# A low-rank feed-forward and the attention behind it: who computes the low parts of ctx, when the second half is turned, and what waits for both halves

## The reference

```python
def _L2_ffn_ref(x, A, B, Wr, br):          # H = 8 heads, rank r = 16
    router_logits = jnp.einsum('bsd,hd->bsh', x, Wr) + br
    scores = H * jax.nn.softmax(router_logits, axis=-1)
    low = jnp.einsum('bsd,hrd->bshr', x, A)
    out = jnp.einsum('bshr,hor,bsh->bso', low, B, scores)
    return SCALING * out                    # SCALING = 2

def _L3_xattn_ref(k, q, v):                 # k = v = ctx, q = layernorm(x)
    scores = jnp.einsum('bcn,bcm->bnm', k, q) / jnp.sqrt(jnp.float32(input_dim))
    attn = jax.nn.softmax(scores, axis=-1)
    return jnp.einsum('bnm,bcm->bcn', attn, v)
```

## Time and profile before

| what | value |
|---|---|
| median of the three runs | 1137.8 us (1135.73 to 1139.4) |
| the profiled execution, its own time | 1140.02 us |
| its span, first to last instruction | 1138.2 us |
| PE busy | 958.2 us (84%) |
| DVE busy | 731.0 us (64%) |
| ACT busy | 470.2 us (41%) |
| POOL busy | 407.1 us (36%) |
| mean granted TensorE clock | 0.904 |
| the touched stage | 854 to 988 us of the span |

### The profile page before, as it was taken

One profiled execution on the slowest core, in us unless ns is written; L12 is line 12 of the kernel. 1 busy time (PEld: TensorE's weight loads), 2 busy tenths in 40 slices (PEclk: granted clock), 3 DMA queues, 4 the chain that ended last, 5 costly groups with the idle time before them and its releaser, 6 DMA issues. The chain is left out here.

```text
span 1138.2 us, 15083 instructions
## 1 busy us (share of the span) xinstructions
PE 958.2 (84%) x5011; PEld 632.0 (56%) x5011; DVE 731.0 (64%) x1180; ACT 470.2 (41%) x687; POOL 407.1 (36%) x371
## 2 busy tenths in 40 slices
PE   5888884999999999999846788899887588769997
PEld 2555542756666666664424556444473355447886
DVE  5577557396778687756878953577643788444434
ACT  2355432325666566652345432344402455335130
POOL 5244212205767565642235720100020432137531
PEclk7699875999999999999977898899987799879999
DMA  8000103135987957547112100000003010022001
GB/s 308 1 1 2 57 1 120 53 130 185 345 290 279 385 202 259 203 151 251 60 65 93 56 1 1 20 1 1 1 1 149 0 47 1 1 74 93 19 20 38
DMA packets 33421, 112.70 MB, mean 99 GB/s; under 512 B 4352, under 2 KB 4672, under 8 KB 30656
## 3 DMA queue, kind: packets, MB, share of 16 engines
q1 hardware_dynamic: 25824, 87.08, 20.9%
q0 software_dynamic: 7520, 24.65, 6.4%
HBM read 132.69 MB, written 16.78 MB: 131 GB/s over the span
## 5 line engine op out<-in xcount | busy, mean ns | idle before, releaser
L1200 POOL DMA_INDIRECT f_picks<-f_turn_xn,f_target x47 | 113.4, 2413 | 73.2 <-ACT f_turn_xn L1089 72.9
L1616 PE MATMUL banks<-f_t_dn,f_z 128*128 128x512 f32 x188 | 88.5, 593 | 0.6 <-issue 0.6
L1344 DVE TENSOR_TENSOR f_gu_lo<-f_t_gu,f_gu_hi 128x2048 fp32r<-128x2048 f32 x24 | 55.2, 2298 | 15.7 <-ACT f_gu_hi L1075 13.4
L1194 POOL DMA_INDIRECT f_turn_xn<-f_xn_rows,f_token x47 | 47.6, 1012 | 43.6 <-DVE f_token L1338 18.7
L1344 DVE TENSOR_TENSOR f_xn_lo<-f_t_gu,f_xn_hi 128x2048 fp32r<-128x2048 f32 x23 | 52.7, 2292 | 14.7 <-ACT f_xn_hi L1075 14.7
L106 POOL TENSOR_TENSOR a_ahead_var_eps<-mean_var,eps 128x1 f32<-128x1 f32 x16 | 3.0, 190 | 161.4 <-DVE mean_var L102 161.4
L2341 ACT ACTIVATE a_e<-banks 128x1024 f32<-128x1024 f32 x32 | 32.7, 1023 | 51.8 <-PE banks L2440 51.7
L1082 ACT ACTIVATE f_sil<-banks 128x256 f32<-128x256 f32 x47 | 18.0, 384 | 78.2 <-PE banks L247 78.2
L1075 ACT CAST f_gu_hi<-f_t_gu 128x2048 fp32r x24 | 45.7, 1904 | 10.7 <-DMA f_t_gu<-in_f_gu 8.2
L164 PE MATMUL banks<-ident,f_turn_xn 128*128 128x128 f32 x96 | 21.6, 379 | 33.8 <-DVE f_turn_xn L172 33.8
L1075 ACT CAST f_xn_hi<-f_t_gu 128x2048 fp32r x23 | 43.7, 1902 | 10.6 <-DMA f_t_gu<-in_f_gu 7.9
(11 more groups left out here) (426 smaller groups left out, 2760.7 us busy)
## 6 DMA issues: line engine op xcount, KB each, us to landing
f_t_gu<-in_f_gu SPq DMA_DIRECT2D x47, 1024.0 KB
f_t_dn<-in_f_dn SPq DMA_DIRECT2D x47, 512.0 KB, 4.5
f_t_gu<-f_picks SPq DMA_DIRECT2D x8, 1024.0 KB, 5.1
f_xn_rows<-f_turn_xn SPq DMA_DIRECT2D x9, 256.0 KB, 2.2
x_res<-in_x SPq DMA_DIRECT2D x8, 256.0 KB, 7.6
a_ctx<-in_ctx SPq DMA_DIRECT2D x2, 1024.0 KB, 13.8
a_out_mask<-in_mask SPq DMA_DIRECT2D x1, 2048.0 KB, 16.0
a_ct<-in_ctx_turned SPq DMA_DIRECT2D x4, 512.0 KB, 7.1
```

Source lines behind the costliest of these rows:

```text
L1194: pool.indirect_dma_start(t_rows[:, t % F0_BUFS, :], None, dram["f0_xn_rows"], bass.IndirectOffsetOnAxis(ap=token[:, t:t + 1], axis=0))\
L1200: pool.indirect_dma_start(dram["f0_picks_flat"], bass.IndirectOffsetOnAxis(ap=target[:, t:t + 1], axis=0), t_y[:, t % F0_BUFS, :], None).t ...
L1344: dve.tensor_tensor(t_gu_lo[t % 2], t_gu[:, bass.ds(i, 1), :, :].rearrange("p i c n -> p (i c n)"), t_gu_hi[t % 2].bitcast(F32), ALU.subtr ...
L1616: mm = pe.matmul(ps[:, TY_BANK + t % 2, :], t_zt[:, t % 2, c, :], t_dn[:, t % F0_BUFS, c, :], start=c == 0, stop=c == F0_IC - 1)
```

## The change

Seven edits, all in this stage:

- The second half's turns are threaded into `lower(0)`: batches 4 and 5 are turned ahead of it, batches 6 and 7 between its second and its third chunk of four. ACT's `take_low(0)` goes behind the casts of batches 4 to 7.
- ctx is no longer split by `Weights`: ACT casts piece 0 between `take_low(0)` and `take_logit(1)` and piece 1 between the exponential of the router and `take_low(1)`.
- The low parts of ctx are made by DVE in four units of two batches: `ctx_lo(0)` ahead of the router's softmax, `ctx_lo(1)` behind the widening, `ctx_lo(2)` ahead of `add_low(0)`, `ctx_lo(3)` behind `maximum(0)`. `scores` waits for a unit every second batch.
- The low part of weight B is made by DVE (`subtract`), ahead of the normalization of batch 5, and no longer by POOL.
- The halves of `low` are waited for apart: `times_low(0)`, `times_low(1)`, `low_rest(0)`, and `low_rest(1)` only behind `add_low(0)`.
- `query(0)` goes ahead of `add_low(1)`, and the first query's low part is made by DVE (`first_query_lo`) behind `add_low(1)`.
- SP loads the two ctx pieces without waits between them, and the next stage's weights once the four units are done.

```diff
--- before.py
+++ after.py
@@ -234,6 +234,14 @@
             else:
                 pool.tensor_tensor(lo, self.raw[:, i % 2, 0:src.shape[1]], hi.bitcast(F32),
                                    ALU.subtract).then_inc(self.lo_ready, 1)
+
+    def subtract(self, dve, pieces):
+        for i in pieces:
+            src, hi, lo = self.pieces[i]
+            dve.wait_ge(self.hi_ready, i + 1)
+            dve.wait_ge(self.lo_ready, i)
+            dve.tensor_tensor(lo, self.raw[:, i % 2, 0:src.shape[1]], hi.bitcast(F32),
+                              ALU.subtract).then_inc(self.lo_ready, 1)
 
     def wait(self, pe, i):
         pe.wait_ge(self.lo_ready, i + 1)
@@ -2551,11 +2559,10 @@
         c_hi = sbuf(nc, lay, "a3_c_hi", [P, B, D], F32R)
         c_lo = sbuf(nc, lay, "a3_c_lo", [P, B, D], F32R)
         v = [sbuf(nc, lay, f"a3_v{h}", [P, NC, HT]) for h in range(HALVES)]
-        pieces = []
-        for h in range(HALVES):
-            batches = slice(h * HB, (h + 1) * HB)
-            pieces.append((dram["ctx_rows"][h], chunked(c_hi[:, batches, :]), chunked(c_lo[:, batches, :])))
-        ctx = Weights(core, "a3", pieces, core.raw)
+
+        ctx_loaded = [core.sem(f"a3_ctx_loaded_{h}") for h in range(HALVES)]
+        ctx_hi_ready, ctx_lo_ready = core.sem("a3_ctx_hi_ready"), core.sem("a3_ctx_lo_ready")
+        UNITS, PER_UNIT = 4, B // 4
         v_loaded = [core.sem(f"a3_v_loaded_{h}") for h in range(HALVES)]
         xn = sbuf(nc, lay, "a3_xn", [P, 2, D])
         q_hi = sbuf(nc, lay, "a3_q_hi", [P, 2, D], F32R)
@@ -2596,10 +2603,12 @@
                 sp.dma_start(br[:, :], dram["f2_br"]).then_inc(br_loaded, 16)
 
                 sp.wait_ge(weights.lo_ready, len(weights.pieces))
-                ctx.load(sp)
+                for h in range(HALVES):
+                    sp.dma_start(core.raw[:, h, :], dram["ctx_rows"][h]).then_inc(ctx_loaded[h], 16)
                 for h in range(HALVES):
                     sp.dma_start(chunked(v[h][:, :, :]), dram["ctx_turned"][h]).then_inc(v_loaded[h], 16)
-                ctx.prefetch(sp)
+                sp.wait_ge(ctx_lo_ready, UNITS)
+                core.prefetch(sp, "a3", None)
 
             @block.gpsimd
             def _(pool):
@@ -2616,13 +2625,10 @@
                     pool.tensor_tensor(q_lo[:, b % 2, :], xn[:, b % 2, :], q_hi[:, b % 2, :].bitcast(F32),
                                        ALU.subtract).then_inc(q_lo_ready, 1)
 
-                weights.split_lo(pool, [1])
                 pool.memset(scales[:, :], scale).then_inc(scales_set, 1)
-                ctx.split_lo(pool, [0])
                 pool.wait_ge(scales_set, 1)
                 middle_scale(0)
                 middle_scale(1)
-                query_lo(0)
                 for b in range(B):
                     if b + 1 < B:
                         query_lo(b + 1)
@@ -2630,8 +2636,6 @@
                         ahead.scale(pool, b - 2)
                     if b + 2 < B:
                         middle_scale(b + 2)
-                    if b == 0:
-                        ctx.split_lo(pool, [1])
                 ahead.scale(pool, B - 2)
                 ahead.scale(pool, B - 1)
 
@@ -2653,6 +2657,10 @@
                     if b >= 2:
                         act.wait_ge(scores_done, NC * (b - 1))
                     act.copy(q_hi[:, b % 2, :], xn[:, b % 2, :]).then_inc(q_hi_ready, 1)
+
+                def ctx_hi(h):
+                    act.wait_ge(ctx_loaded[h], 16)
+                    act.copy(chunked(c_hi[:, h * HB:(h + 1) * HB, :]), core.raw[:, h, :]).then_inc(ctx_hi_ready, 1)
 
                 def exp(j):
                     act.wait_ge(shift_ready, j + 1)
@@ -2673,18 +2681,18 @@
                 weights.split_hi(act, [1])
                 act.wait_ge(br_loaded, 16)
                 take_logit(0)
+                turned.act(act, range(HB, B))
                 take_low(0)
-                turned.act(act, range(HB, B))
+                ctx_hi(0)
                 take_logit(1)
                 act.wait_ge(shifted_ready, 1)
                 act.activation(weight[:, :, :], weight[:, :, :], ACT.Exp).then_inc(weight_exp, 1)
+                ctx_hi(1)
                 take_low(1)
-                ctx.split_hi(act, [0])
                 for h in range(HALVES):
                     act.wait_ge(lt_ready, h + 1)
                     act.copy(lt_hi[:, rows_of(h)], lt[:, rows_of(h)]).then_inc(lt_hi_ready, 1)
                 query_hi(0)
-                ctx.split_hi(act, [1])
                 for j in range(A3_JOBS):
                     exp(j)
                     if j >= 1:
@@ -2720,6 +2728,30 @@
                     dve.tensor_scalar(xn[:, b % 2, :], core.x[:, b, :], middle.mean(b), rstd[:, b:b + 1],
                                       ALU.subtract, ALU.mult).then_inc(xn_ready, 1)
 
+                def first_query_lo():
+                    dve.wait_ge(q_hi_ready, 1)
+                    dve.tensor_tensor(q_lo[:, 0, :], xn[:, 0, :], q_hi[:, 0, :].bitcast(F32), ALU.subtract)\
+                       .then_inc(q_lo_ready, 1)
+
+                def ctx_lo(u):
+                    h, part = divmod(u, UNITS // HALVES)
+                    batches = slice(u * PER_UNIT, (u + 1) * PER_UNIT)
+                    dve.wait_ge(ctx_hi_ready, h + 1)
+                    dve.tensor_tensor(chunked(c_lo[:, batches, :]),
+                                      core.raw[:, h, part * PER_UNIT * D:(part + 1) * PER_UNIT * D],
+                                      chunked(c_hi[:, batches, :]).bitcast(F32), ALU.subtract).then_inc(ctx_lo_ready, 1)
+
+                def times_low(h):
+                    dve.wait_ge(low_ready, h + 1)
+                    dve.wait_ge(wide_turned, h + 1)
+                    dve.tensor_tensor(lt[:, rows_of(h)], low[:, rows_of(h)], ps[:, G_BANK + h, :],
+                                      ALU.mult).then_inc(lt_ready, 1)
+
+                def low_rest(h):
+                    dve.wait_ge(lt_hi_ready, h + 1)
+                    dve.tensor_tensor(lt_lo[:, rows_of(h)], lt[:, rows_of(h)], lt_hi[:, rows_of(h)].bitcast(F32),
+                                      ALU.subtract).then_inc(lt_lo_ready, 1)
+
                 def maximum(j):
                     dve.wait_ge(scores_done, j + 1)
                     dve.tensor_reduce(shift[:, j:j + 1], ps[:, S_BANK + j % 2, :], AX.X, ALU.max,
@@ -2743,7 +2775,10 @@
 
                 turned.dve(dve, range(0, 2))
                 weights.first_lo(dve)
-                turned.dve(dve, range(2, B))
+                turned.dve(dve, range(2, HB + 1))
+                weights.subtract(dve, [1])
+                turned.dve(dve, range(HB + 1, B))
+                ctx_lo(0)
                 dve.wait_ge(logits_turned, 1)
                 after(dve.tensor_reduce(col[:, :], by_row(), AX.X, ALU.max))
                 dve.tensor_tensor(weight[:, :, :], by_row(), by_batch(col), ALU.subtract)\
@@ -2758,21 +2793,21 @@
                     batches = slice(h * HB, (h + 1) * HB)
                     w = weight[:, batches, :].unsqueeze(3).broadcast_to([P, HB, F2_H, F2_R])
                     dve.tensor_copy(wide[:, batches, :, :], w).then_inc(wide_ready, 1)
-                dve.wait_ge(low_ready, HALVES)
-                for h in range(HALVES):
-                    dve.wait_ge(wide_turned, h + 1)
-                    dve.tensor_tensor(lt[:, rows_of(h)], low[:, rows_of(h)], ps[:, G_BANK + h, :],
-                                      ALU.mult).then_inc(lt_ready, 1)
-                for h in range(HALVES):
-                    dve.wait_ge(lt_hi_ready, h + 1)
-                    dve.tensor_tensor(lt_lo[:, rows_of(h)], lt[:, rows_of(h)], lt_hi[:, rows_of(h)].bitcast(F32),
-                                      ALU.subtract).then_inc(lt_lo_ready, 1)
+                ctx_lo(1)
+                times_low(0)
+                times_low(1)
+                low_rest(0)
+                ctx_lo(2)
                 add_low(0)
+                low_rest(1)
+                query(0)
                 add_low(1)
-                query(0)
+                first_query_lo()
                 for j in range(A3_JOBS):
                     b, n = divmod(j, NC)
                     maximum(j)
+                    if j == 0:
+                        ctx_lo(3)
                     if j >= 1:
                         invert(j - 1)
                         divide(j - 1)
@@ -2789,8 +2824,8 @@
 
             @block.tensor
             def _(pe):
-                def product(out, cols, h):
-                    for c in range(NC):
+                def product(out, cols, h, chunks=range(NC)):
+                    for c in chunks:
                         mm = matmul_split(pe, out, a_hi[:, c, cols], a_lo[:, c, cols],
                                           hi[:, c, rows_of(h)], lo[:, c, rows_of(h)], c == 0, c == NC - 1)
                     return mm
@@ -2799,8 +2834,10 @@
                     pe.wait_ge(turned.lo_ready, HB * (h + 1))
```

(16 more changed lines are left out.)

## The result

| | before | changed kernel |
|---|---|---|
| median of the four runs of each | 1138.6 us (1135.73 to 1141.37) | 1121.2 us (1116.63 to 1125.67) |
| ratio | | 0.9837, 95% interval 0.9801 to 0.9873 |
| profiled execution, own time; span | 1140.02; 1138.2 us | 1125.67; 1123.9 us |
| stages ahead (same code) | 853.97 us | 856.08 us |
| touched stage, first DVE instruction to the next stage's | 134.90 us | 120.81 us |

The account below looks back on a forecast made before the run. The feed-forward was taken as bound by a chain from engine to engine, no engine full. Terms -10.0 (to scores(0)), +1.2 and -4.2 sum to -13.0 us, from 1137.8 to 1124.8 us; own range 1121 to 1128, reaching 1120.5 to 1130.5.

Parts of the forecast that it names:

- Parts 1 and 2: Turns amid lower(0), with PE's clock staying full through logits(1): the router's first DVE step 5.0 us earlier.
- rival of a falling clock: logits(1) runs at 1.2 GHz as before, costing 2.4 us, total 1127.2 us; chance 16%.
- Part 3: Casts and low parts of ctx put into waits: hidden, margins 0.55 us (cast) and 0.7 us (unit 0); a unit 1.22 us.
- Parts 4 and 5: ACT's cast and POOL's subtraction out of the way of f_lt's splitting, ahead of low_output(0): -0.9 and -3.9 us.
- Part 6: From low_output(0) to scores(0): -0.5 us for matmuls at full clock, +0.4 for low_rest(1) holding POOL; scores(0) 10.0 us earlier.
- Part 7: Unit 3 of ctx's low parts behind maximum(0) in the attention: +1.2 us, bounds 0.7 and 2.3.
- Part 8: POOL's second subtraction gone from the attention, between maximum(4) and maximum(8): -4.2 us, bounds -2.5 and -4.5.

Follow-up runs that it names:

- e5: Kernel before with one line moved: ACT casts ctx piece 0 ahead of take_logit(1), POOL still making the low part; ratio 0.9934 to the kernel before.
- e8: Changed kernel plus a useless POOL subtraction of two unrelated SBUF tiles ahead of its first scaling; low_rest(0) 4.54 us instead of 0.69, touched stage 125.15 us.
- e12: Changed kernel unaltered, third set of timings; 1125.5 us against 1142.2 for the kernel before, ratio 0.9835; touched stage 122.58 us.
- e9: Changed kernel plus two useless POOL memsets ahead of its first scaling; touched stage 120.76 us, stage behind 149.69 us.
- e10: Changed kernel plus one useless DVE subtraction of 448 columns ahead of the stage's last add; 1125.1 us, ratio 0.9879 to the kernel before.
- e1: Changed kernel unaltered, run again for a second set of timings; 1125.6 us against 1139.9 for the kernel before, ratio 0.9882.
- e4: Kernel before with only the second half's turns put amid lower(0) and take_low(0) behind the casts; ratio 0.9967 to the kernel before.
- e11: Changed kernel plus two useless DVE subtractions of 1024 columns ahead of the stage's last add; 1129.5 us, ratio 0.9908 to the kernel before.
- e7: Changed kernel with add_low(1) and query(0) ahead of low_rest(1), and ctx_lo(3) ahead of the first maximum; 1121.1 us against 1138.1 for the kernel before, ratio 0.9849.

## Why the prediction was wrong

Parts 1 and 2, -5.0 for the router: -5.05 in the profile, -5.02 and -4.94 when put back or made alone. The rival of a falling clock didn't come: `logits(1)` ran at 1.00 (rows above). Part 3: the cast and unit 0 were hidden, with margins of 0.57 and 0.74 us (0.55 and 0.7 worked out); a unit takes 1.22 us, as interpolated. Parts 4 and 5, -4.8: -4.89 in e5. In the changed kernel `low_output(0)` came 37.93 - 27.96 = 9.97 us earlier, 9.8 worked out. Part 6: `scores(0)` -10.4, not -10.0. `low_rest(1)` did hold POOL (0.47 - 0.19 = 0.28 us, taken 0.4). Part 7, +1.2 for unit 3: 0.89. Part 8, -4.2: from 12.52 to 7.91 us, -4.6; I had followed these jobs to 8.3, and the lower bound that I gave, -4.5, was passed by 0.1. Together the touched stage came to -14.1, 1.1 more than the sum; all three terms, parts 6, 7 and 8, erred to the same side. The mechanism of the touched stage was right in each part. Two things in the working don't hold as written. The rule of two SBUF inputs is said to speak for part 8 too, but the division has one tensor input (see e8); its price rested on the rows, and came. And the range's own terms, taken all at once, give 1121.8 to 1129.9, so the 1121 given for "not all at once" lies outside even that, and the reach to 1120.5 had no term under it.

The step that failed stands behind the sum: "From then on the loop is as before, and so is the next stage". The loop was, to 0.02 us; the next stage was not. It took 2.3 us less in the first profile (149.33 to 147.01), and 2.0 to 2.4 less in the two other profiles of the changed kernel. With it the sum would have been -13.0 - 2.3 = -15.3, or -16.4 with the stage's measured 14.1. The prediction puts that term at nothing with the reason that the stage's weights land far ahead, and it costs the clock only where the change has instructions. What the runs showed in its place: the stage behind takes 146.9 to 149.7 us, in step with when its clock comes up, 3.3 to 6.7 us after its start. With e12's slower touched stage among them, the three profiles of the changed kernel give (14.1 + 14.1 + 12.3) / 3 = 13.5 us there and 2.3 behind, 15.8 in all; the three sets of timings gave 17.4, 14.3 and 16.6, 16.1 on average.

The second step is "1.8 us to either side by which the runs shown differ from their median". Three runs showed 3.7 us of width; 24 runs later showed 11.7 (1134.29 to 1146.03), from stages whose code is the same. The rest of the first result's 17.4 us, over these 15.8, is within that. Which part of that spread a set of four runs catches is luck: the second set's 14.3 would have lain within the range. Whether the 2.3 us behind would stay in a mean over many runs is open, as e9 and e10 show. Why the stages ahead take 849 us in one run and 857 in the next was not taken apart: their granted clock differs from run to run (0.82 to 0.91 in the first two stretches of 150 us), but what sets it stays open.

## What to carry to other kernels

A subtraction of two SBUF tiles on DVE and one on POOL don't run side by side: look for a DVE instruction that takes 4.5 us where its like takes 0.7, and move the long one into a wait, even if nothing else changes (e5: 4.9 us at `low_output(0)` and 3.9 at the stage's end, for one line moved). Where PE's clock rises and falls in a stage, a later stage of unchanged code can take 2 to 3 us more or less (147.29 in e1, 149.69 in e9, behind touched stages of one length), so give a forecast that much room to both sides, and measure small edits by the touched stage's length in the trace. Before taking a spread from three runs, ask for more of them.

## What the runs showed of the hardware

- One stage's code took 146.91 to 149.69 us in 14 profiles, in step with when its clock came up to 1.00 after its start: 3.3 us (e5) to 6.7 us (e4, e9). In one profile each, 0.6 us of work added ahead of it (e10) and 2.5 us (e11) ended in the same sum of the two stages, 270.86 and 270.84 us.
- Relative to the touched stage's start the clock's first rise falls nearly alike from run to run, though the stages ahead differ by 8 us: by the same working it comes 11.6 and 11.5 us after the start in the two profiles of the kernel before, and 11.5, 11.8 and 13.4 us in the three of the changed kernel. Why, no run here shows.
- Small POOL operations are held as well: a 128x1 addition takes 0.19 us in e7 and 0.47 in the changed kernel, where it starts within DVE's `low_rest(1)` and ends with it.
- DVE's subtraction of 1024 columns takes 1.214 to 1.226 us (the four of the changed kernel). The Trainium skill (VectorE: DVE Perf Modes, The TRN2 errata) gives (N + 151) / 0.96 ns for an fp32 add of two tensors, by which an estimate for N = 1024 is 1.224 us; the trace agrees.
